# A 512-column row norm becomes four columns and comes back through TensorE

## The reference, cut to what matters

```
x = x + mlp(x)                      # 512 -> 2048 -> 512, part of it by expert
x = x + x @ W_subject + b
# third block, per sequence:
gated = x * sigmoid([x, ema(x)] @ Wg + bg)
mod   = 0.5 + sigmoid(gelu(x @ Wn1 + bn1) @ Wn2 + bn2)      # 4 values per token
traces = 4 moving averages over time of gated * mod[d]
temporal = sum_d blend[d] * traces[d]
gate = sigmoid(temporal @ Wtemp + btemp)
out  = (gelu(x @ Wsoma + bsoma) * gate) @ Wout
x = x + (out - mean(out)) / sqrt(var(out) + 1e-5) * gamma + beta   # over 512 channels
# fourth block:
x = x + x @ W_expert + b
```

## Time and profile before

| | |
|---|---|
| median of 3 runs | 1403.28 us (1402.93 to 1405.6) |
| the profiled execution, its own time | 1402.93 us |
| its span, first to last instruction | 1401.2 us |
| PE busy | 1361.5 us, 97% of the span |
| DVE busy | 782.6 us, 56% (in the rounds about 64 us of each 70 to 71) |
| ACT busy | 481.0 us, 34% |
| mean granted TensorE clock | 0.991 |

### The profile page before, as it was taken

How to read it: one execution, slowest core, us unless ns; L and a number is a source line. 1 busy time by engine, 2 the same in 40 slices (tenths; PEclk the granted TensorE clock), 3 DMA queues, 4 the chain that set the end, 5 groups by cost and what they waited for, 6 DMA issues and landing times.

```text
span 1401.2 us, 15112 instructions
## 1 busy us (share of the span) xinstructions
PE 1361.5 (97%) x5888; PEld 1108.7 (79%) x5888; DVE 782.6 (56%) x1035; ACT 481.0 (34%) x799; POOL 133.6 (10%) x170
## 2 busy tenths in 40 slices
PE   7999989999999999999999999799999999999988
PEld 6888878888788888788887887668787878787876
DVE  3334333332343332341321584999898989898993
ACT  4443233332232332332321222242424242424253
POOL 5000100000100000100000221012100220032000
PEclk9999999999999999999999999989999999999999
DMA  5422441501632501721322956421232123211201
GB/s 123 134 77 83 129 149 67 180 2 68 169 110 90 158 18 66 205 73 61 112 75 72 211 178 188 133 91 61 91 121 91 61 91 120 91 61 61 91 0 60
DMA packets 68375, 140.89 MB, mean 101 GB/s; under 512 B 7328, under 2 KB 19616, under 8 KB 64336
## 3 DMA queue, kind: packets, MB, share of 16 engines
q1 hardware_dynamic: 60784, 115.66, 26.3%
q0 software_dynamic: 6944, 23.23, 6.1%
q10 hardware_dynamic: 576, 1.05, 0.2%
HBM read 86.85 MB, written 53.05 MB: 100 GB/s over the span
## 4 chain that ended last, share of the span: by engine, by line
PE 88%; DMA 5%; DVE 4%; ACT 2%; issue 0%; SPq 0%; DVEq 0%; ACTq 0%
PE bank L977 29%; PE bank L978 29%; PE bank L979 29%; DMA wout_dram<-stage_lo 1%; DMA stage<-in_exp_w 1%; DMA l3w_dram<-stage_lo 1%; DMA wg_dram<-stage_lo 1%; DVE drive L1400 1%; PE bank L1151 1%; PE bank L1044 1%; DVE temporal L1410 0%; DVE drive L1385 0%; DMA stage_early<-in_fc_w 0%; DVE x_hl L1244 0%; DMA x_slot<-x2hl_dram 0%
## 5 line engine op out<-in xcount | busy, mean ns | idle before, releaser
L1244 DVE TENSOR_TENSOR h_hl<-bank,h_hl 128x512 fp32r<-128x512 f32 x128 | 88.7, 693 | 441.0 <-ACT h_hl L845 441.0
L977 PE MATMUL bank<-x_hl,wa 128*128 128x512 f32 x512 | 203.3, 397 | 18.5 <-DVE h_hl L1244 10.1
L978 PE MATMUL bank<-x_hl,wa 128*128 128x512 f32 x512 | 202.0, 394 | 0.0
L979 PE MATMUL bank<-x_hl,wa 128*128 128x512 f32 x512 | 201.8, 394 | 0.0
L977 PE MATMUL bank<-h_hl,wa 128*128 128x512 f32 x512 | 199.5, 390 | 0.0
L978 PE MATMUL bank<-h_hl,wa 128*128 128x512 f32 x512 | 199.4, 390 | 0.0
L979 PE MATMUL bank<-h_hl,wa 128*128 128x512 f32 x512 | 199.2, 389 | 0.0
L841 ACT ACTIVATE bank<-bank,small_sb 128x512 f32<-128x512 f32 x128 | 84.1, 657 | 211.0 <-PE bank L979 210.9
L845 ACT ACTIVATE h_hl<-bank 128x512 fp32r<-128x512 f32 x128 | 76.7, 599 | 212.8 <-PE bank L979 212.2
L977 PEld LDWEIGHTS bank<-x_hl,wa 128*128 128x128 f32 x512 | 97.7, 191 | 42.4 <-DVE h_hl L1244 11.3
L979 PEld LDWEIGHTS bank<-x_hl,wa 128*128 128x128 f32 x512 | 97.8, 191 | 20.8
(11 more groups left out here) (149 smaller groups left out, 2314.8 us busy)
## 6 DMA issues: line engine op xcount, KB each, us to landing
x_slot<-x2hl_dram SPq DMA_DIRECT2D x32, 513.0 KB, 4.6
x2hl_dram<-x_hl POOLq DMA_DIRECT2D x28, 512.0 KB, 9.8
stage<-in_l_w SPq DMA_DIRECT2D x32, 256.0 KB, 3.2
x_dram<-x_raw SPq DMA_DIRECT2D x8, 1024.0 KB, 6.2
xt<-x_dram SPq DMA_DIRECT2D x8, 1024.0 KB, 5.8
mod_t<-mod_dram POOLq DMA_DIRECT2D x8, 1024.0 KB, 4.9
l3w_hl<-l3w_dram SPq DMA_DIRECT2D x16, 512.0 KB, 7.1
x_raw<-in_x SPq DMA_DIRECT2D x7, 1024.0 KB, 7.5
```

What stands on the lines that cost most here:

```text
L977: eng.matmul(ps, w_hi, x_hi, start=first, stop=False)
L978: eng.matmul(ps, w_hi, x_lo, start=False, stop=False)
L979: return eng.matmul(ps, w_lo, x_hi, start=False, stop=final)
L1244: return eng.tensor_tensor(lo, raw, hi.bitcast(F32), ALU.subtract)
```

## The change

The sum of squares is made with the roles swapped: `ss` runs four matmuls with a 128x128 chunk of `sumsq` as weights and a single column of ones as the moving operand. The result is 128 tokens (on partitions) by 4 columns. The square root on ACT and the reciprocal on DVE then handle 128x4. To bring the numbers back to the layout with tokens along the free axis, DVE multiplies the identity by each of the four columns (`diag`, 4 x 128x128), and PE multiplies ones by each `diag` chunk (`rb`, four matmuls of 128 columns) into bank 6, from which `z_of` reads.

In the lists: PE gets `rb(r-2)` between `n1(r)` and `gate(r, 0)`; `mo(r)` moves from inside `gate(r, 0)` to behind it; `rb(6)` stands ahead of `te(7)`, `rb(7)` between `l3(6, 2)` and `l3(6, 3)`. DVE's `rows_rstd(r-1)` moves ahead of `traces_d(r, 3)` (in round 1 ahead of `traces_c(1, 3)`), and the two halves of `temporal_low` stand together. On ACT `temporal_hi(r, 2)` moves ahead of `h1_of(r+1)`.

```diff
-                eng.activation(rstd[:, :], SS_BANK[:, :], ACT.Sqrt, bias=eps_sb[:, 0:1],
+                eng.activation(std[:, :], SS_BANK[:, 0:TOK // P], ACT.Sqrt, bias=eps_sb[:, 0:1],
...
             for r in range(2, NT):
                 h1_of(r)
-                temporal_hi(r - 1, 2)
                 temporal_hi(r - 1, 3)
...
-                    if m == 0 and c == 0 and i > 1:
-                        mo(i)
...
-                eng.matmul(SS_BANK[:, :], ones[:, :], sumsq[:, :], start=True, stop=True).then_inc(s_pe["SS"], 1)
+                for q in range(TOK // P):
+                    mm = eng.matmul(SS_BANK[:, q:q + 1], sumsq[:, q * P:(q + 1) * P], ones[:, 0:1],
+                                    start=True, stop=True)
+                mm.then_inc(s_pe["SS"], 1)
+
+            def rb(i):
+                if i < LAST:
+                    on.wait_ge(s_gated, KC * (i + 1) + 3)
+                else:
+                    on.wait_ge(s_z, KC * LAST)
+                for q in range(TOK // P):
+                    on.wait_ge(s_diag, (TOK // P) * i + q + 1)
+                    mm = eng.matmul(RB_BANK[:, q * P:(q + 1) * P], ones[:, :], diag[:, q * P:(q + 1) * P],
+                                    start=True, stop=True)
+                mm.then_inc(s_pe["RB"], 1)
...
                 if r > 1:
                     n1(r)
+                if r > 1:
+                    rb(r - 2)
                 gate(r, 0)
-                if r == 1:
+                if r > 1:
+                    mo(r)
+                else:
                     gate(r, 1)
...
+            rb(LAST - 1)
             for m in range(KC):
                 te(LAST, m)
...
             l3(LAST - 1, 2)
+            rb(LAST)
             l3(LAST - 1, 3)
...
             def rows_rstd(i):
                 on.wait_ge(s_std, i + 1)
-                eng.reciprocal(rstd[:, :], rstd[:, :]).then_inc(s_rstd, 1)
+                eng.reciprocal(rstd[:, :], std[:, :]).then_inc(s_rstd, 1)
+                on.wait_ge(s_rstd, i + 1)
+                on.wait_ge(s_id, 3)
+                if i:
+                    on.wait_ge(s_pe["RB"], i)
+                for q in range(TOK // P):
+                    eng.tensor_scalar(diag[:, q * P:(q + 1) * P], ident[:, :], rstd[:, q:q + 1], None, ALU.mult
+                                      ).then_inc(s_diag, 1)
...
             def z_of(i, m):
-                on.wait_ge(s_rstd, i + 1)
+                on.wait_ge(s_pe["RB"], i + 1)
...
-                eng.scalar_tensor_tensor(o, o, gamma_sb[:, m:m + 1], rstd[:, :], ALU.mult, ALU.mult
+                eng.scalar_tensor_tensor(o, o, gamma_sb[:, m:m + 1], RB_BANK[:, :], ALU.mult, ALU.mult
...
                 traces_a(r, 3)
                 traces_b(r, 3)
                 traces_c(r, 3)
+                rows_rstd(r - 1)
                 traces_d(r, 3)
-                temporal_low(r, 0)
-                if r < LAST:
-                    rows_rstd(r - 1)
-                temporal_low(r, 2)
-
-            rows_rstd(LAST - 1)
+                temporal_low(r)
+
             norm_of(LAST - 1)
```

More of the change, by code:

```diff
@@ L129, in build @@
         trace_last = const("trace_last", KC * TAUS)
+        std = const("std", TOK // P)
+        rstd = const("rstd", TOK // P)
         zeros = const("zeros", 2)
@@ L132, in build @@
         ident = const("ident", P)
-        rstd = const("rstd", TOK)
+        diag = const("diag", TOK)
         stage_hi = nc.alloc_sbuf_tensor_at("stage_hi", [P, TOK], F32R, offset=constants_at[0] - 4 * TOK)
@@ L182, in build @@
         s_pe = {k: sem("s_pe_" + k) for k in
-                ("L1", "N1", "SO", "MO", "WG", "TE", "OU", "SS", "L3")}
+                ("L1", "N1", "SO", "MO", "WG", "TE", "OU", "SS", "RB", "L3")}
         s_x2free = sem("s_x2free")
@@ L209, in build @@
         s_rstd = sem("s_rstd")
+        s_diag = sem("s_diag")
         s_z = sem("s_z")
@@ L324, in l3_bank @@
             return bank[((7, 4, 7, 4) if i < LAST else (1, 2, 3, 5))[m]]
-        SS_BANK = bank[0]
+        SS_BANK, RB_BANK = bank[0], bank[6]
         def x2_at(i, c):
@@ L805, in rows_std @@
                 if i:
[L806 to L809, removed]
-                eng.activation(rstd[:, :], SS_BANK[:, :], ACT.Sqrt, bias=eps_sb[:, 0:1],
+                    on.wait_ge(s_rstd, i)
+                eng.activation(std[:, :], SS_BANK[:, 0:TOK // P], ACT.Sqrt, bias=eps_sb[:, 0:1],
                                scale=1.0 / DIM).then_inc(s_std, 1)
@@ L912, in _ @@
             soma_of(1, 3)
-            temporal_hi(1, 0)
-            temporal_hi(1, 1)
+            for m in range(SH):
+                temporal_hi(1, m)
             for r in range(2, NT):
                 h1_of(r)
-                temporal_hi(r - 1, 2)
                 temporal_hi(r - 1, 3)
@@ L943, in _ @@
                 soma_of(r, 3)
-                temporal_hi(r, 0)
-                temporal_hi(r, 1)
-            temporal_hi(LAST, 2)
+                for m in range(SH):
+                    temporal_hi(r, m)
             temporal_hi(LAST, 3)
@@ L956, in _ @@
                 spikes_hi(LAST, m)
-            on.wait_ge(s_z, KC * LAST)
-            eng.activation(rstd[:, 0:1], eps_sb[:, 0:1], ACT.Sqrt).then_inc(s_chain, 1)
+            on.wait_ge(s_rstd, LAST)
+            eng.activation(std[:, 0:1], eps_sb[:, 0:1], ACT.Sqrt).then_inc(s_chain, 1)
             y_of(LAST - 1, 0)
@@ L1431, in traces_d, with temporal_low @@
                 add_of(i, c, 3)
[L1433 to L1436, removed]
+            def temporal_low(i):
+                for p in (0, 2):
+                    on.wait_ge(s_temphi, KC * i + p + 2)
+                    low_part(temporal_lo[:, p:p + 2, :], temporal[:, p:p + 2, :], ts_hi[:, p:p + 2, :]
+                             ).then_inc(s_templo, 2)
             def spikes(i, m):
@@ L1571, in _ @@
             x2_of(LAST, 1)
-            temporal_low(0, 0)
-            temporal_low(0, 2)
+            temporal_low(0)
             x2_of(LAST, 2)
@@ L1600, in _ @@
             traces_b(1, 3)
+            rows_rstd(0)
             traces_c(1, 3)
             traces_d(1, 3)
-            temporal_low(1, 0)
-            rows_rstd(0)
-            temporal_low(1, 2)
+            temporal_low(1)
             for r in range(2, NT):
```

## The result

The changed kernel takes 1412.4 us (median of 5 runs, 1411.64 to 1413.32) where the kernel before takes 1403.28: 1.0059 times as long, 95% interval 1.0044 to 1.0074, or +8.3 us by the ratio. It is slower, and by a little less than half of what was forecast. A later execution of it that took 2795.59 us stands in none of the figures. The profiled execution has a time of its own of 1413.11 us and a span of 1411.1, 9.9 us more than the span before.

What follows compares the result with a forecast made beforehand. PE's list was taken as the bound, busy 97% of the span. Terms 11.0 + 5.8 + 1.0 - 1.6 + 1.0 + 0.6 = +17.8 on 1402.93 gave 1420.7, 1421 as median; range 1408 to 1432.

Steps and rivals of the forecast that it cites:

- The pair of load and matmul: In `ss` and `rb` on PE: each weight load with its matmul takes 0.229 us, eight make 1.83 us.
- rival 1: Cheaper pairs in `ss` and `rb`: loads run one behind the other at 0.107 to 0.15 us; total 1406; chance 0.18.
- The 81 ns for a pair: Skill page's figure for steady loads and 128-column matmuls on PE: 0.65 us for `ss`, total about 1 us over before.
- The clock in `te(7)`: Ahead of `te(7)`, `rb(6)` cuts the standstill to about 1.4 us, so the clock is kept: -1.6 us.
- `mo` at 0: In rounds, `mo` behind `gate(r, 0)` starts `drive` 5.9 us later, but 1.4 us of cover remain: cost 0.
- the moved `rows_rstd`: Delays `traces_d(7, 3)` by some 1.2 us; `temporal_low` waits longer for ACT, so `te(7)` starts as before relative to `so_pair(7)`.
- The tail: After `ss(7)`: `rb(7)` stands behind `l3(6, 2)`, so `z_of(7, 0)` comes 4.7 us after instead of 4.1, +0.6.
- DVE's relief: Shorter reciprocal less `diag` gives DVE about 2.1 us back in each round, with nobody waiting for it: gain 0.
- 2: Rival on PE's pairs: only the array's columns count and loads cost no PE time; about -4.9, 1398; chance 0.04.
- 3: Rival on PE's pairs: load and matmul run serially, 0.35 and 0.46 us a pair; total 1440; chance 0.08.
- 4: Rival in rounds: DVE becomes the bound, `mod_t` lands after 9.7 us, `ss` waits 3.4 us; +20, 1441; chance 0.06.
- 5: Rival in rounds: the clock falls because one-column matmuls hardly use the array, 1.6 us at twelve places; 1440; chance 0.04.

Runs made afterwards that it cites:

- the run for tiles 6 and 7: Kernel before, with the new normalizing for tiles 6 and 7 alone and `mo` left inside `gate(r, 0)`: 1401.7 us, ratio 0.9991.
- the four `rb`: Changed kernel with `rb(6)` issued four times over ahead of `te(7)`: 1411.2 us, ratio 1.0055.
- both runs with fillers: Useless matmuls ahead of `ss(0)` and in the standstill before `te(7)`: in the kernel before, 1400.92 us; with new normalizing for tiles 6 and 7 alone, 1398.81 us.

## Why the prediction was off

The direction was right, and so was the main place, PE's list in the rounds; the size was not: +17.8 forecast, +8.3 measured, less than half.

- **The pair of load and matmul** is the step that failed. "So load and start by themselves fill 0.22 to 0.23 us, and shortening the matmul between need not shorten that distance" read a limit out of a coincidence: that a load starts with the matmul ahead of it, and the next matmul just behind its end, does not say that the load sets their distance. A pair takes 0.10 (`ss`) and 0.11 us (`rb`), as in rival 1, down at the bound that the two load rows gave. The terms: `rb` 11.0 forecast, 5.4 measured; `ss(1)` to `ss(6)` 5.8 forecast, 0.2 measured; `ss(0)` +1.0 forecast, where 8 x 0.37 were taken and 8 x 0.21 came out, and with `so_pair(1)` behind it 8.8 us in place of 8.6; `ss(7)` +1.0 forecast, below 0.1 measured. `rb` alone in the kernel before shows +5.9.
- **The 81 ns for a pair** in the Trainium skill (page "TensorE: Matmul & The Clock Gate", section "Back-to-back issue gap") were nearer to the measured 0.10 to 0.11 us than the row as I read it. The estimate from them, 0.65 us for `ss`, was low: 0.81 to 0.90 came out.
- **The clock in `te(7)`**: -1.6 forecast, +0.8 in the profiled execution and +1.0 in the second profile. "1.4 is below 1.6, so I take the clock as kept" took two rows for a threshold. Six profiles with 2.0 to 2.5 us of waiting behind `rb(6)` fell on both sides. The standstill that was left was also longer than 1.4 us: 1.3 ahead of `rb(6)`, whose input the prediction took to be there, and 2.5 behind it, since `rb` took 0.9 and not 1.8, and `te(7)` started late.
- **`mo` at 0** was right in rounds (6.8 us waits on DVE, about 7 forecast, none of `ss`) and wrong at the end of round 7. I carried the lateness up to `sum_squares` and stopped; behind it DVE's wait for ACT ahead of `temporal_low(7)`, 1.65 us in the trace of before, was all the cover there was. The prediction did use that wait, for the moved `rows_rstd`, and rightly by itself: 1.0 us of delay. But the modulation's 1.9 us draw on it too, and the two together took the 1.65 and 1.7 more. Two delays, each put at nothing against the same wait, were not nothing together. Putting `mo` back gives the 1.7 back.
- **The tail**: +0.6 forecast, -0.4 measured, which is rival 1's figure, as it must be with `rb` at 0.9. That the reciprocal's gain is eaten by the place of `rb` in PE's list is right: three matmuls earlier in the list were worth another 0.6 us in the run for tiles 6 and 7.
- **DVE's relief**: `diag` takes 0.87 us for four (1.0 forecast), the reciprocal 0.17; nobody was waiting in rounds. Right there; at the end of round 7 these 1.0 us are part of the late start above.
- **In no term, and not the change's**: in the profiled execution six `n1` spent 1.2 us more, waiting for their slots. In the second profile of the same kernel they took what they did before, 17.3 us, and over the other runs 16.8 to 18.3 (the one with `rows_rstd` late left aside, where PE waits for `diag` behind `n1`).
- **Rivals**: 1 was right in its mechanism and, at 1406, short of the time, mostly by `te(7)`: its late start of 1.7 us, and a clock that it too put at -1.6; 2 and 3 are put away by the pair, 4 by the list of waits (mod_t landed at 5.3 us in the median), 5 by the clock of 1.00 in rounds with twice the pairs.

## What to carry to other kernels

Where one engine's list is the time, a change that moves work onto it costs the work, however much it frees elsewhere; put the new form only where that engine stands still anyway. The length of an instruction's record is not the distance at which the next can follow: here a load's record of 192 ns stood against a distance of 111, and the difference between the records of two sizes, 104 ns, was the better guide. A lateness has to be followed to the end of the program, not to the first slack that covers it, and delays that draw on the same slack have to be added before they are held against it.

## What the runs showed that was not expected

- Weight loads of 128 columns in plain float32, recorded at 186 to 192 ns, follow each other with a short matmul between them every 0.10 to 0.11 us at full clock, be it of one column or of 128, and every 0.21 us at half (eight in 1.70 us).
- The distance of split matmuls is 0.229 us at full clock and 0.43 at half. The pairs, of plain float32 and with load records as long, follow at half that distance, so it is hardly the loads that set it; what does was not tried.
- After a standstill broken by one `rb` the clock fell in four profiles of six. With the array kept busy by useless matmuls it held in each of the three profiles made (the four `rb`, both runs with fillers), and keeping it up for `ss(0)` and `te(7)` is a gain that was there in the kernel before, 1.8 us of it measured.
